# Attention with the output transposed: fp32 exponentials as the moving operand, in two 64-column halves of the array

## The reference, cut to what matters

```
x = queries                              # (4, 1024, 128) fp32
x = x + attn(layernorm(x))               # 16 heads of 64, rotary on the first 32 of each 64
x = x + lowrank_ffn(layernorm(x))        # 128 -> 32 -> 512, gelu, 512 -> 32 -> 128

q, k, v = split_heads(x @ Wq), split_heads(x @ Wk), split_heads(x @ Wv)
q, k = rope(q), rope(k)
attn = softmax(q @ k.T / 8)              # (4, 16, 1024, 1024)
out  = (attn @ v).merge_heads() @ Wout + bout
```

## Time and profile before

| what | value |
|---|---|
| median of 3 runs | 1656.41 us (1650.69 to 1668.54) |
| profiled execution, its own time | 1647.82 us |
| its span, first to last instruction | 1646.0 us |
| granted TensorE clock, mean | 0.968 of full speed |
| busy share PE / DVE / ACT / POOL | 88% / 89% / 80% / 68% |
| one pass of the hardware loop | 95.4 us |

### The profile page before, as it was taken

One profiled execution on the slowest core, in us unless ns is written; L12 is line 12 of the kernel. 1 busy time (PEld: TensorE's weight loads), 2 busy tenths in 40 slices (PEclk: granted clock), 3 DMA queues, 4 the chain that ended last, 5 costly groups with the idle time before them and its releaser, 6 DMA issues.

```text
span 1646.0 us, 45814 instructions
## 1 busy us (share of the span) xinstructions
PE 1450.6 (88%) x15353; PEld 1178.5 (72%) x15353; DVE 1459.8 (89%) x1893; ACT 1312.8 (80%) x2696; POOL 1122.2 (68%) x1012
## 2 busy tenths in 40 slices
PE   3888898998989899898989989898998989899897
PEld 1567686776868677686867768686776768677684
DVE  6898997989889898989989898998989899899878
ACT  3787787887879788787978878797887878789675
POOL 2498866758576675858667585866758586676951
PEclk9899998999999999999999999999999999999999
DMA  5321031220203122020312202031221203122001
GB/s 165 79 53 41 14 79 28 53 54 19 70 19 79 28 53 54 16 73 19 79 28 53 54 20 76 12 79 28 53 54 33 64 12 79 28 53 53 1 2 52
DMA packets 60692, 78.62 MB, mean 48 GB/s; under 512 B 17476, under 2 KB 27208, under 8 KB 60200
## 3 DMA queue, kind: packets, MB, share of 16 engines
q1 hardware_dynamic: 59008, 74.42, 17.8%
q10 hardware_dynamic: 1448, 1.00, 0.2%
HBM read 5.79 MB, written 2.10 MB: 5 GB/s over the span
## 4 chain that ended last, share of the span: by engine, by line
PE 52%; DVE 28%; issue 13%; POOL 4%; ACT 2%; DMA 1%; DVEq 1%; SPq 0%; ACTq 0%; POOLq 0%
PE O L414 10%; DVE PR L660 10%; DVE MS L648 10%; PE O L416 9%; PE S L394 9%; PE S L393 9%; PE M L436 8%; PE TILE L342 2%; DVE STAGE L550 2%; PE TILE L323 2%; DVE T L546 2%; PE TILE L329 2%; DVE QK L1101 1%; ACT MS L515 1%; ACT PF L531 1%
## 5 line engine op out<-in xcount | busy, mean ns | idle before, releaser
L660 DVE TENSOR_TENSOR PR<-PF 128x1024 f16<-128x1024 f32 x512 | 699.6, 1369 | 107.9 <-ACT PF L531 104.2
L531 ACT ACTIVATE PF<-S 128x512 f32<-128x512 f32 x1024 | 619.3, 605 | 174.5 <-PE S L394 159.7
L414 PE MATMUL O<-V,PF 128*128 128x129 f16 x4096 | 591.3, 223 | 132.9 <-DVE PR L660 98.3
L515 ACT ACTIVATE MS<-M 128x512 f16<-128x512 f32 x1012 | 612.4, 606 | 29.4 <-issue 29.4
L416 PE MATMUL O<-V,PR 128*128 128x129 f16 x4096 | 591.5, 221 | 0.0
L394 PE MATMUL S<-QK 65*128 65x256 f16 x2048 | 520.3, 278 | 0.0
L393 PE MATMUL S<-QK 128*128 128x256 f16 x2048 | 516.7, 277 | 3.2 <-DMA QK<-MN 2.8
L414 PEld LDWEIGHTS O<-V,PF 128*128 128x128 bf16 x4096 | 403.9, 99 | 157.8 <-DVE PR L660 114.2
L416 PEld LDWEIGHTS O<-V,PR 128*128 128x128 f16 x4096 | 407.0, 99 | 116.0 <-issue 7.0
L648 DVE TENSOR_TENSOR MS<-MS 128x2048 f16<-128x2048 f16 (+3 forms) x512 | 433.6, 847 | 28.5 <-ACT MS L515 21.7
L705 POOL TENSOR_TENSOR ON<-OS 128x128 f32<-128x128 f32 x256 | 226.7, 886 | 325.3 <-ACT OS L507 325.0
(11 more groups left out here) (88 smaller groups left out, 1079.3 us busy)
## 6 DMA issues: line engine op xcount, KB each, us to landing
QK<-STAGE SPq DMA_DIRECT2D x384, 128.0 KB, 2.5
V<-VS SPq DMA_DIRECT2D x64, 260.0 KB, 2.3
X<-in_L_attn_queries SPq DMA_DIRECT2D x4, 512.0 KB, 12.7
out<-X SPq DMA_DIRECT2D x8, 256.0 KB, 2.3
WRAW<-in_L_attn_Wkv SPq DMA_DIRECT2D x1, 1024.0 KB, 9.3
ROPE<-in_rope SPq DMA_DIRECT2D x1, 1024.0 KB, 12.5
QK<-MN SPq DMA_DIRECT2D x64, 2.0 KB, 1.9
WRAW<-in_L_attn_Wq ACTq DMA_DIRECT2D x1, 512.0 KB, 4.5
```

The lines of the kernel that those rows point to most:

```text
L414: e.matmul(O[bank][:, qt, 0:VW], hi[:, 2 * at + 1:2 * (at + P):2], vals, start=(s == 0 and j == 0), stop=False, skip_group_check=True)
L515: e.activation(MS[:, (place_u // HALF) % 2, q, c * 512:(c + 1) * 512], bank, ACT.Copy, scale=-1.0 / MSCALE).then_inc(unit_copied, 1)
L531: e.activation(PF[:, (2 * k + s // 2) % 4, (s % 2) * 512:(s % 2 + 1) * 512], S[s % 2][:, :, :].rearrange("p a b -> p (a b)"), ACT.Exp, sca ...
L660: e.tensor_tensor(PR[:, buf, :], PF[:, buf, :], PF[:, buf, :].bitcast(BF16)[:, 1:2048:2], ALU.subtract).then_inc(rest_made, 1)
```

## The change

- `pe_values` turns the product round. V (fp32, 128 keys by 64) is now the stationary operand, and the fp32 exponentials `PF` are the moving one, 512 queries at a time. The first 512 queries go to partitions 0 to 63 of the PSUM bank, the others to partitions 64 to 127, so each uses a half of the array's columns. The two-part splits of the exponentials (`dve_rest`, `PR`) and of V go away, and so does V's extra column. The output is transposed already, so `turn` goes away.
- A step `t` is now 128 keys by all 1024 queries of one head: 32 steps in a pass, each twice the work of one `s` before.
- The sums of the exponentials are made by adds: POOL adds pairs of `PF` blocks in place (`pool_sum`, four of 128x1024 for each head), DVE three more for each head (`dve_sum`), and a product with ones (`den_tile`, four fp32 products of 32 columns) gives them in PSUM. From there they go over ACT, a DMA, a DVE reciprocal, a DMA to DRAM and a DMA back (`den_over`), and DVE multiplies them in (`dve_norm`), for two heads at once, 128x1024.
- The maxima are read by DVE straight from PSUM, 128x1024 at a time (`dve_max`); the ACT copies to `MS` and the folds go away. The unit is now two matmuls of 512 columns into one PSUM buffer, for which PE waits each step.
- The output projection is 16 fp32 products of 64 rows by 128 columns for each pair of heads (`out_tiles`), with weights fetched anew in each pass (`weights_over`). In the tail, `down2` is an fp32 product of 32 columns for each quarter, and `rest` goes away.

```
-        V = sb("V", [P, GH, KT * VP], F16)
+        V = sb("V", [P, GH, KT * DH], F32)
...
-            for j in range(4):
-                kt = half * 4 + j
-                at = j * QW + qt * P
-                vals = V[:, h, kt * VP:kt * VP + VW]
-                e.matmul(O[bank][:, qt, 0:VW], hi[:, 2 * at + 1:2 * (at + P):2], vals,
-                         start=(s == 0 and j == 0), stop=False, skip_group_check=True)
-                mm = e.matmul(O[bank][:, qt, 0:VW], PR[:, buf, at:at + P], vals,
-                              start=False, stop=(half == 1 and j == 3), skip_group_check=True)
+            e.wait_ge(exped, 2 * n + 2)
+            for z in range(2):
+                mm = e.matmul(O[h % 2][DH * z:DH * z + DH, :], V[:, h, kt * DH:(kt + 1) * DH],
+                              PF[:, t % SLOTS, z * HALF:(z + 1) * HALF], start=(kt == 0), stop=(kt == KT - 1),
+                              skip_group_check=True)
+            mm.then_inc(pv_done, 1)
...
+        def pe_unit(e, u, place, q, bank):
+            for c in range(2):
+                mm = e.matmul(bank[:, c * 512:(c + 1) * 512], QHL[:, place, q:N:KT],
+                              KHH[:, place, c * 512:(c + 1) * 512], start=True, stop=True)
+            mm.then_inc(unit_made, 1)
...
+        def pe_step(e, it, t):
...
+            pe_tiles(e, it, t)
+            pe_scores(e, it, t)
...
+                e.wait_ge(max_read, it.step(u))
+                pe_unit(e, it.step(u), place, q, M)
...
+        def den_tile(e, q, bank):
+            e.wait_ge(summed, 4 * q + 4)
+            for hh in range(2):
+                for z in range(2):
+                    s = 2 * hh + z
+                    mm = e.matmul(T[bank][32 * s:32 * s + 32, :], ONES[:, :], SUM[:, hh, z * HALF:(z + 1) * HALF],
+                                  start=True, stop=True)
...
+        def dve_max(e, u, head, place, q, bank):
+            e.wait_ge(unit_made, u + 1)
+            e.tensor_reduce(MX[:, place % 2, q:q + 1], bank[:, :], AX, ALU.max).then_inc(max_read, 1)
...
+        def dve_sum(e, nth, head, h, second):
+            e.wait_ge(two_summed, 2 * nth + 2)
+            if not second:
+                wait(e, den_copied, head // 2)
+                e.tensor_tensor(SUM[:, h % 2, :], PF[:, 0, :], PF[:, 2, :], ALU.add).then_inc(summed, 1)
+            else:
+                e.tensor_tensor(PF[:, 4, :], PF[:, 4, :], PF[:, 6, :], ALU.add).then_inc(four_summed, 1)
+                e.wait_ge(four_summed, head + 1)
+                e.tensor_tensor(SUM[:, h % 2, :], SUM[:, h % 2, :], PF[:, 4, :], ALU.add).then_inc(summed, 1)
...
+        def pool_sum(e, t, steps):
+            e.wait_ge(exped, 2 * steps)
+            e.wait_ge(pv_done, steps - 1)
+            e.tensor_tensor(PF[:, t % SLOTS, :], PF[:, t % SLOTS, :], PF[:, t % SLOTS + 1, :],
+                            ALU.add).then_inc(two_summed, 1)
```

More of the change, by code:

```diff
@@ L67 @@
[L67 to L75, removed]
+PROJ_AT = (2, 4, 5, 7, 8, 10, 11, 14, 15, 16, 17, 18)
+DEN_AT = {3: 1, 19: 0}
+INVERT_AT = {6: 1, 22: 0}
@@ L78, in tiles_of @@
 def tiles_of(first, last):
     out = []
[L81 to L94, removed]
+    for t in range(STEPS):
+        if t in PROJ_AT and not last:
+            out.append((t, "proj", PROJ[PROJ_AT.index(t)]))
+        if first and t in TURN_X0_AT:
+            out.append((t, "turn_x", (0, PRE_CHUNKS + TURN_X0_AT.index(t))))
+        if last and t in TURN_X_AT:
+            out.append((t, "turn_x", (1, TURN_X_AT.index(t))))
+        if last and t in DOWN_AT:
+            out.append((t, "down", DOWN_AT.index(t)))
+        if t in DEN_AT and not (first and DEN_AT[t]):
+            out.append((t, "den", DEN_AT[t]))
+        if t in OUT_AT and not (first and OUT_AT[t]):
+            out += [(t, "out", (OUT_AT[t], z)) for z in range(2)]
@@ new lines, in pe_scores @@
+        def pe_scores(e, it, t):
+            n, h, kt = it.step(t), t // KT, t % KT
+            keys = slice(kt * P, (kt + 1) * P)
+            if kt == 0:
+                e.wait_ge(max_row, 16 * (it.i * GH + h + 1))
+            for z in range(2):
+                rows = slice(z * HALF, (z + 1) * HALF)
+                wait(e, exped, 2 * n + z - 1)
+                e.matmul(S[:, rows], KHH[:, h, keys], QHL[:, h, rows], start=True, stop=False)
+                e.matmul(S[:, rows], KL1[0:DH + 1, h, keys], QHM[0:DH + 1, h, rows],
+                         start=False, stop=True).then_inc(scored, 1)
@@ L769, in sp_iteration @@
                     continue
+                if what in ("sums", "inverse", "spread"):
+                    if not (it.first and h):
+                        den_over(sp, what, it.pair(h))
+                    continue
+                if what == "wo":
+                    weights_over(sp, it, h)
+                    continue
                 if (it.first if h == GH - 1 else it.last):
@@ L819, in _ @@
             loop(sp, sp_iteration)
+            for what in ("sums", "inverse", "spread"):
+                den_over(sp, what, PAIRS - 1)
             for c in range(FC):
@@ L1127, in _ @@
             for c in range(2, FC):
-                rest(c)
                 if c == 4:
```

655 lines of the change are left out of this document (289 added, 366 removed).

## The result

The changed kernel takes 1705.6 us (1704.8 to 1707.0), the one before, on the same chip, 1660.8. The span of the profiled execution goes from 1646.0 to 1704.3 us, +58.3, against a forecast of +70. (The profiled execution of the kernel before, 1647.8 us, is shorter than each of its four runs, 1650.7 to 1668.5, and by the medians the step is 45 us. What follows compares the two profiles.)

What follows compares the result with a forecast made beforehand. PE was taken as first bound, DVE's order before it as second. A pass of 90.7 + 2.6 + 1 + 5.5 = 99.8 us against 95.4 gives +70, 1718 x 1.005 = 1727 us; forecast range 1640 to 1830, 8-in-10 range 1585 to 1950.

Steps and rivals of the forecast that it cites:

- PE's own work, 90.7: PE in one pass: values, width changes, scores, units, projections, ones products and output projection sum to 90.7 us, against 84.4 before.
- The fp32 price: Value products on PE: a 512-column fp32 product is two records of 0.43 us, so 0.86 us.
- the full overlap of the halves: Value products on PE: the two column halves work at the same time, so values cost 27.5 us a pass, not 55.
- The width change: PE in each step: going from full width to column halves and back costs 0.24 us, 7.7 us a pass.
- The 0.04 us window of the earlier trace: Source-view window of the kernel before, read as one half's matmul passing a waiting matmul of the other half.
- rival B: Value products on PE: the halves don't pass each other, values take 41.3 us a pass, 1950 us in all; chance 0.13.
- The gap at the edge stays: Loop's edge on PE: the idle gap once a pass remains, 2.6 us.
- The clock's term: PE over one pass: the granted clock costs 1 us.
- Waits, 5.5: PE waiting for other engines in a pass: 3 us for DVE between maxima plus 2.5 us for POOL.
- Step 9, forecast at 1.5: PE's stall at step 9, from DVE's rotary tile and two adds between maxima: about 1.5 us a pass.
- the 2.5 us for late POOL adds: Between steps 2 and 15: POOL's rotary additions delay adds that DVE, then PE, wait for; 2.5 us, from 0 to 9.
- Head and tail, 0 (-2 to +6): Outside the passes: some 15 us of DVE residuals go, about 11 us for the last sums come; taken as 0.

Runs made afterwards that it cites:

- e2: Changed kernel with both value products of a step put in the same column half: 2032.1 us, pass 120.2.
- e3: Changed kernel with the values of two steps issued together, so half as many changes of array width: 1717.7 us, ratio 1.0322 to the kernel before.
- e4: Changed kernel with the same products in more, shorter matmuls (scores in 128-column, values in 256-column pieces): 1769.3 us.
- e1: Changed kernel with DVE's row maxima taken over the first 512 keys only, leaving out work: 1637.7 us, pass 94.9.
- e12: Changed kernel with e9's edit and DVE's third add of each head left to the ones product: 1655.4 us, ratio 0.9998 to the kernel before.
- e9: Changed kernel with the scaling of the maxima (L595) moved from DVE to ACT: 1681.4 us.
- e5: Changed kernel with the output projection of step 12 moved to step 13: 1754.6 us, pass 102.4.
- e6: Changed kernel with e5's edit and the Q and K projection tiles moved earlier: 1840.4 us, pass 109.2.
- e8: Changed kernel with e6's order and e9's edit together: 1741.4 us, ratio 1.0492 to the kernel before.
- e10: Changed kernel with e9's edit, DVE's second adds and what follows one step later, output projection at step 13, neighbouring tiles later: 1836.4 us, ratio 1.1034 to the kernel before.
- e13: e12 with the output projection at step 13 and the tiles of steps 14 to 18 one step later: 1654.5 us, ratio 1.0009 to the kernel before.
- e11: Changed kernel with POOL's pair adds on the first 512 queries only, leaving out work: 1658.8 us.

## Why the prediction was right, by its own steps

**PE's own work, 90.7: right,** 91.5 measured. The fp32 price (0.86 a product), the full overlap of the halves (e2) and the width change (0.24 forecast, 0.25 by e3) all hold. The 0.04 us window of the earlier trace rows was the row that decided against rival B, and it pointed the right way.

**The edge and the clock, 2.6 + 1: 2.1 too much.** "The gap at the edge stays" is the step that failed. The changed kernel's PE has half the instructions, its body stays loaded and the gap is 0 (e4 brings it back). The clock's term was 1 and is 1.5, in a stretch behind a wait, so it hangs on that wait (e1, e12).

**Waits, 5.5: 6.0 measured, from partly other sources.** Step 9, forecast at 1.5, is the 1.98 before step 10's unit. Steps 25 and 26, at 0.9, are the waits at steps 26 and 27, 1.1 of idle time together. Steps 1 and 13, at 0.4, don't show, and step 21 has 0.3. Not forecast: the 1.97 before the output projection, a bank that I didn't follow, and the scaling L595, which stood in the diff and which I didn't price at all. Against that, the 2.5 us for late POOL adds were the right mechanism at the wrong address: POOL's own adds came near the undisturbed rate (2.42; 2.7 forecast), and the price fell on DVE's. I had listed DVE's adds at 1.2 to 2.3 in the sum, and had not asked what a disturbed one does in its place in the order.

**Head and tail, 0 (-2 to +6): too low.** They are +7: 1 less ahead of the first value product, 8 more behind the last. The chain that ended last has this between the last values and the last output projection:

```profile
1650.27 2.36 POOL PF L670
1652.65 1.24 DVE PF L605
1653.91 1.24 DVE SUM L607
...
1659.76 2.28 DMA RT<-DS
...
1665.57 2.85 DMA RB<-den
```

The last output projection starts at 1669.8, 19.4 us behind the last value product; in the kernel before it starts at 1607.05, 6.9 behind. The step is 12.5, where I had 11: the three DMAs with their issues and the reciprocal alone are 10.6 (1657.9 to 1668.45). So that price was nearly right. What failed is what I set against it: I let 15 us for the residuals that go, less what ACT takes of them, cancel the 11, but from that projection to the end there are 34.5 us instead of 38.9, only 4.4 less. Why no more was saved there wasn't tested.

**The sum.** A pass was put at 90.7 + 2.6 + 1 + 5.5 = 99.8 and is 91.5 + 0 + 1.5 + 6.0 = 99.0. That it comes so near is in part luck: the edge, 2.6 too much, covers 1.8 too little in the three other terms. The growth was put at 4.4 a pass, 70 us; it is 51, both for the 0.8 of this sum and because the pass of 95.4 that I took for all 16 was one of the shortest. The 7 us of head and tail make up for a part of that, again by luck, and the span grows by 58. So 12 of the 21 us by which the forecast was high are a difference of two errors. The other 9 are the factor 1.005, which I took from the scatter of the kernel before: the changed kernel scatters by 2 us only, and its profiled execution (1706.2) is its median to within 1 us.

**The direction.** Against the pass of the earlier trace rows, PE, the first bound, got 7.1 us more work (91.5 against 84.4), the vanished edge gave 2.8 of it back, and the waits for DVE, 6.5 then, are 6.0 now although DVE has 247 us less to do in the run. With those waits thinned out (e12) the loss of 50 us is gone, but nothing is gained: PE's longer work has used up what the freed engines gave.

## What to carry to other kernels

Price the bound engine's work by spacings of the same kind of record in the trace, and take two halves of the array as concurrent, fp32 too, with 0.25 us (as measured here) for each change from full width and back. Then list, for each step, the operations of VectorE and GpSimd that exclude each other, tiny ones as well, and count each one at the other engine's length: fewer of them helped (24 us in e9, 26 more in e12), while moving work about cost 49 and 135 us against the changed kernel (e5, e6), 60 and 155 against e9, whose edit they share (e8, e10), and changed nothing against e12 (e13). And start a forecast from the mean of many passes, not from one that happened to be picked: here the two differ by 0.6 us, 16 times. A change that halves an engine's instructions may also win back the loop's edge.

## What the hardware showed unexpectedly

- Products in different column halves don't wait for each other: the first records of both start within 0.02 us, although the first product, two records long, is issued ahead of the second.
- A VectorE operation on 128x8 elements, 0.17 us alone, lasted up to 2.36 us, the length of GpSimd's add.
- A loop whose body has about 940 TensorE records a pass has a gap of 2.5 to 3.0 us at its edge and 2.54 MB on the instruction queue; one with about 450 has neither.
- After a wait of 1.98 us TensorE ran at its lower level for its next records (1.97 against 1.08 us for the same four). In e9 the same wait was there in each pass, and yet some passes (96.6) were 1.7 us shorter than others (98.3). In e11 a wait of 1.96 us was followed by records at full speed in one pass and not in another. What decides is not settled here.
